# POOL waits for the landing of every third send in a two-layer mixture-of-experts kernel

## What is computed

```python
x = x + 0.5 * _L0_ffn_ref(_layernorm(x), ...)    # pass 0: each token to one of 8 experts
x = x + _L0_attn_ref(_layernorm(x), ...)         # conv, two running means, a gelu layer
x = x + 0.5 * _L0_ffn_ref(_layernorm(x), ...)    # pass 1: the same 8 experts
x = x + 0.5 * _L1_ffn_ref(_layernorm(x), ...)    # 16 experts, 320 places each
x = x + _L1_attn_ref(_layernorm(x), ...)         # a linear scan over the 4096 rows' blocks
x = x + 0.5 * _L1_ffn_ref(_layernorm(x), ...)    # the same 16 experts
```

## Time and profile before

| | us |
|---|---|
| timed runs, median of 3 | 703.73 |
| timed runs, lowest and highest | 702.21, 706.83 |
| profiled execution, first to last instruction | 768.4 |
| PE busy in it | 639.2 |
| POOL busy in it, 377 instructions | 367.9 |

### The profile page before, as it was taken

One profiled execution on the slowest core, in us unless ns is written; L12 is line 12 of the kernel. 1 busy time (PEld: TensorE's weight loads), 2 busy tenths in 40 slices (PEclk: granted clock), 3 DMA queues, 4 the chain that ended last, 5 costly groups with the idle time before them and its releaser, 6 DMA issues.

```text
span 768.4 us, 13116 instructions
## 1 busy us (share of the span) xinstructions
PE 639.2 (83%) x3647; PEld 490.1 (64%) x3647; DVE 449.7 (59%) x1882; ACT 329.6 (43%) x1038; POOL 367.9 (48%) x377
## 2 busy tenths in 40 slices
PE   4451799999989999857997679999997975989996
PEld 4441798986767658756986654576663764466664
DVE  6620456696899987622444330567763875166674
ACT  2220455747866544322553200645531841074551
POOL 0466346345312173554444555366661146445676
PEclk9665899999999999977999769999998997899999
DMA  9661466435103114444767212533397011455330
GB/s 302 234 176 57 124 193 197 114 93 175 61 1 81 43 41 112 140 116 130 189 206 239 69 41 67 177 97 119 110 283 158 13 37 49 116 152 169 99 98 15
DMA packets 85879, 93.95 MB, mean 122 GB/s; under 512 B 12152, under 2 KB 65307, under 8 KB 85552
## 3 DMA queue, kind: packets, MB, share of 16 engines
q1 hardware_dynamic: 73648, 74.23, 33.9%
q0 software_dynamic: 10880, 15.07, 5.9%
q10 hardware_dynamic: 1280, 3.81, 1.5%
HBM read 64.18 MB, written 33.76 MB: 127 GB/s over the span
## 4 chain that ended last, share of the span: by engine, by line
PE 52%; DVE 13%; issue 11%; POOL 7%; another core or an unknown queue 7%; DMA 5%; ACT 3%; SPq 1%; ACTq 0%; DVEq 0%; POOLq 0%
PE ps L901 8%; PE ps L921 8%; PE ps L894 8%; PE ps L821 5%; PE ps L829 5%; POOL y L1610 4%; PE ps L843 3%; PE ps L736 2%; PE ps L876 2%; PE ps L869 2%; POOL xs L1606 2%; PE ps L884 1%; PE ps L778 1%; PE ps L908 1%
## 5 line engine op out<-in xcount | busy, mean ns | idle before, releaser
L1606 POOL DMA_INDIRECT xs<-X,IDX x128 | 125.4, 980 | 143.5 <-issue 70.4
L1499 ACT ACTIVATE ht<-ps,CL 128x128 f32<-128x128 f32 x336 | 93.7, 378 | 136.1 <-PE ps L821 68.1
L1610 POOL DMA_INDIRECT y<-yt,xi x84 | 83.3, 992 | 107.3 <-DVE yt L1242 96.7
L829 PE MATMUL ps<-W,ht 128*128 (+1 forms) x672 | 94.3, 294 | 12.1 <-ACT ht L1499 8.8
L821 PE MATMUL ps<-xt,w1s 128*128 128x128 f32 x672 | 91.8, 291 | 11.4 <-DVE xt L1236 6.2
L829 PEld LDWEIGHTS ps<-W,ht 128*128 128x128 f32 x672 | 86.9, 205 | 18.8 <-issue 17.7
L821 PEld LDWEIGHTS ps<-xt,w1s 128*128 128x128 f32 x672 | 86.4, 205 | 14.0 <-DVE xt L1236 6.5
L921 PE MATMUL ps<-MT,KC 128*128 128x512 f32 x136 | 68.4, 662 | 9.6 <-remote 5.0
L1236 DVE COPY xt<-ps 128x128 f32<-128x128 f32 x84 | 24.1, 287 | 72.9 <-remote 38.4
L921 PEld LDWEIGHTS ps<-MT,KC 128*128 128x128 f32 x136 | 27.9, 212 | 43.9 <-issue 31.5
L811 PE MATMUL ps<-KC,xh 128*128 128x128 f32 x84 | 24.9, 296 | 35.0 <-issue 16.6
(11 more groups left out here) (214 smaller groups left out, 1310.9 us busy)
## 6 DMA issues: line engine op xcount, KB each, us to landing
w1s<-in_w SPq DMA_DIRECT2D x84, 256.0 KB
W<-in_w1x SPq DMA_DIRECT2D x17, 512.0 KB
wx<-in_w1x SPq DMA_DIRECT2D x15, 512.0 KB
X<-y SPq DMA_DIRECT2D x24, 256.0 KB
xs<-ZX SPq DMA_DIRECT2D x32, 185.0 KB
xi<-xs SPq DMA_DIRECT2D x84, 66.0 KB
x<-xs SPq DMA_DIRECT2D x22, 148.0 KB
X<-in_x SPq DMA_DIRECT2D x8, 264.0 KB
```

Source lines behind the costliest of these rows:

```text
L829: r = e.matmul(ps[TILE_BANKS[i % len(TILE_BANKS)]][:, 0:P], HT[i % NHT][:, c, :], W02[:, bass.ds(r0 * F + c * P, P)], start=(c == 0), stop ...
L1499: r = e.activation(HT[i % NHT][:, c, :], ps[TILE_BANKS[i % len(TILE_BANKS)]][:, c * P:(c + 1) * P], ACT.Gelu, bias=CL[:, bass.ds(r0 * 4 + ...
L1606: return e.indirect_dma_start(dst, bass.IndirectOffsetOnAxis(ap=IDX[:, n:n + 1], axis=0), X[:, n, 0:w], None, bounds_check=hi, oob_is_err= ...
L1610: return e.indirect_dma_start(dst, bass.IndirectOffsetOnAxis(ap=ix, axis=0), src, None, bounds_check=hi_home, oob_is_err=False, engine_sem ...
```

## The change

A step called rest is put into POOL's list behind every third send of a row of sends (a row is a stretch of sends and homes without much between them), 40 times in all. A rest makes POOL wait until the send that it issued last has landed. Rests stand behind sends 2 and 5; 8, 11, 14, 17, 20, 23, 26 and 29; 37 and 42; 50; 52, 54, 57, 58, 59 and 61; 64 and 67; 68, 71, 74, 77, 80, 83, 86, 89 and 92; and 98, 101, 104, 107, 110, 113, 116, 119, 122 and 125. Nothing else is added, no instruction is moved on any engine, and the other four lists are the same.

```diff
     "pool": """
-send.0 send.1 send.2 send.3 send.4 send.5 send.6 send.7 send.8 send.9 send.10 send.11 send.12 send.13 send.14 send.15 send.16 send.17 send.18 send.19
+send.0 send.1 send.2 rest.0 send.3 send.4 send.5 rest.1 send.6 send.7 send.8 rest.2 send.9 send.10 send.11 rest.3 send.12 send.13 send.14 rest.4
...
             POOL.wait_ge(sem("pad"), 1)
+            sends, landed = {}, None
             for stage, i in ORDER["pool"]:
-                if stage == "ppow":
+                if stage == "rest":
+                    POOL.wait_ge(sem(landed[0]), landed[1])
+                elif stage == "ppow":
...
-                        send(xs0[p], hi_tile[p], n, ROW).then_inc(sem(f"sent{g - GP.index(p)}"), 16)
+                        name = f"sent{g - GP.index(p)}"
+                        send(xs0[p], hi_tile[p], n, ROW).then_inc(sem(name), 16)
                     else:
...
+                        name = "sentx"
                         send(xs1[p - 2], hi_expert, n, ROWX, sem("issued")).then_inc(sem("sentx"), 16)
+                    sends[name] = sends.get(name, 0) + 16
+                    landed = name, sends[name]
                 elif stage == "home":
...
                     home(y[i >= PASS0[1]], yt[:, :], XI[i % NXI][:, R_ID:ROW].bitcast(U32)).then_inc(sem(f"home{i % NHS}"), 16)
+                    landed = f"home{i % NHS}", turns(i, NHS)
```

More of the change, by code:

```diff
@@ L210 @@
[L210 to L213, removed]
@@ new lines @@
+tturn.73 tup.71 tup.72 tdown.70 tturn.74 tdown.71 tdown.72 tturn.75 tup.73 tturn.76 tup.74 tup.75 tturn.77 tdown.73 tdown.74 tdown.75 pturn.14
+pturn.15 tturn.78 tup.76 pscore.16 tup.77 tdown.76 tturn.79 tup.78 tdown.77 qrank.0 tturn.80 pturn.16 tdown.78 tturn.81 tup.79 tup.80 tturn.82 tup.81
+pscore.17 tdown.79 tturn.83 tdown.80 tdown.81 tup.82 tup.83 tdown.82 qrank.1 tdown.83 pturn.17 pscore.18 pturn.18 pscore.19 qrank.2 warm.0 qrank.3
+pscore.20 warm.1 pturn.19 pturn.20 pturn.21 pscore.21 pscore.22 pscore.23 qrank.4 qrank.5 warm.2 warm.3 qrank.6 warm.4 warm.5 qrank.7 warm.6 warm.7
@@ new lines @@
+warm.8 warm.9 warm.10 warm.11 warm.12 warm.13 warm.14 warm.15 warm.16 warm.17 warm.18 warm.19 warm.20 warm.21 warm.22 warm.23 warm.24 warm.25 warm.26
+warm.27 warm.28 warm.29 warm.30 warm.31 warm.32 warm.33 warm.34 eturn.0 eturn.1 eup.0 eup.1 eup.2 eup.3 eup.4 eup.5 edown.0 eup.6 eup.7 eturn.2
+eback.0 edown.1 eturn.3 eup.8 eup.9 eup.10 eup.11 eup.12 eback.1 eup.13 eup.14 eup.15 eturn.4 edown.2 eup.16 eup.17 eturn.5 eup.18 eback.2 eup.19
+edown.3 eup.20 eturn.6 eback.3 edown.4 eup.21 eup.22 eup.23 eback.4 eup.24 eup.25 eup.26 eup.27 eturn.7 edown.5 eup.28 eup.29 eback.5 edown.6 eturn.8
@@ new lines @@
+rturn.1 rB.0 rB.1 rC1.0 rC2.0 rturn.2 rturn.3 rC1.1 rB.2 rC2.1 pturn.22 pscore.24 rC1.2 rturn.4 rB.3 qrank.8 pturn.23 rC2.2 pscore.25 rC1.3 rB.4
+pturn.24 rturn.5 rC2.3 qrank.9 rC1.4 pscore.26 pturn.25 rturn.6 rB.5 qrank.10 rC2.4 pscore.27 rB.6 pturn.26 rC1.5 rC2.5 rturn.7 pscore.28 qrank.11
+rC1.6 rB.7 rC2.6 qrank.12 pturn.27 pturn.28 pscore.29 rC1.7 pscore.30 rC2.7 qrank.13 qrank.14 pturn.29 pscore.31 qrank.15 warm.50 warm.51 warm.52
+warm.53 warm.54 warm.55 warm.56 warm.57 warm.58 warm.59 warm.60 warm.61 warm.62 warm.63 warm.64 warm.65 warm.66 warm.67 eturn.16 eup.64 eup.65 eup.66
@@ new lines @@
+egexp.31 erela.63""",
+    "pool": """
+send.0 send.1 send.2 rest.0 send.3 send.4 send.5 rest.1 send.6 send.7 send.8 rest.2 send.9 send.10 send.11 rest.3 send.12 send.13 send.14 rest.4
+send.15 send.16 send.17 rest.5 send.18 send.19 send.20 rest.6 send.21 send.22 send.23 rest.7 send.24 send.25 send.26 rest.8 send.27 send.28 send.29
+rest.9 send.30 send.31 home.0 home.1 home.2 home.3 home.4 home.5 home.6 home.7 home.8 home.9 home.10 home.11 home.12 home.13 home.14 home.15 home.16
+home.17 home.18 home.19 apow1.0 home.20 home.21 apow1.1 home.22 home.23 home.24 home.25 home.26 home.27 home.28 apow2.0 apow2.1 home.29 home.30
@@ new lines @@
+home.31 home.32 home.33 home.34 home.35 home.36 apow3.0 home.37 home.38 apow3.1 home.39 home.40 apow1.2 apow1.3 apow1.4 apow1.5 apow2.2 apow1.6
+apow1.7 apow2.3 apow3.2 apow2.4 apow2.5 apow3.3 apow2.6 ppow.0 apow2.7 apow3.4 apow3.5 send.32 send.33 send.34 apow3.6 send.35 send.36 send.37 rest.10
+send.38 send.39 ppow.1 send.40 send.41 send.42 rest.11 send.43 apow3.7 send.44 send.45 send.46 ppow.2 send.47 ppow.3 send.48 send.49 send.50 rest.12
+send.51 home.41 home.42 home.43 home.44 send.52 rest.13 send.53 home.45 home.46 home.47 send.54 rest.14 send.55 send.56 send.57 rest.15 home.48
@@ new lines @@
+home.49 send.58 rest.16 home.50 home.51 send.59 rest.17 send.60 home.52 send.61 rest.18 send.62 send.63 home.53 home.54 home.55 home.56 home.57
+home.58 home.59 home.60 home.61 home.62 home.63 home.64 home.65 home.66 home.67 home.68 home.69 home.70 home.71 home.72 home.73 home.74 home.75
+home.76 home.77 send.64 rest.19 send.65 send.66 send.67 rest.20 home.78 home.79 home.80 home.81 home.82 home.83 send.68 rest.21 send.69 send.70
+send.71 rest.22 send.72 send.73 send.74 rest.23 send.75 send.76 send.77 rest.24 send.78 send.79 send.80 rest.25 send.81 send.82 send.83 rest.26
@@ new lines @@
+send.84 send.85 send.86 rest.27 send.87 send.88 send.89 rest.28 send.90 send.91 send.92 rest.29 send.93 send.94 send.95 epow.0 epow.1 epow.2 epow.3
+epow.4 epow.5 ehome.0 ehome.1 epow.6 ehome.2 epow.7 ehome.3 ehome.4 epow.8 ehome.5 epow.9 ehome.6 epow.10 epow.11 ehome.7 ehome.8 epow.12 epow.13
+ehome.9 epow.14 ehome.10 ehome.11 epow.15 ehome.12 ehome.13 ehome.14 ehome.15 send.96 send.97 send.98 rest.30 send.99 send.100 send.101 rest.31
+send.102 send.103 send.104 rest.32 send.105 send.106 send.107 rest.33 send.108 send.109 send.110 rest.34 send.111 send.112 send.113 rest.35 send.114
@@ L316 @@
+send.115 send.116 rest.36 send.117 send.118 send.119 rest.37 send.120 send.121 send.122 rest.38 send.123 send.124 send.125 rest.39 send.126 send.127
+epow.16 epow.17 epow.18 epow.19 epow.20 epow.21 ehome.16 ehome.17 epow.22 ehome.18 epow.23 ehome.19 ehome.20 epow.24 ehome.21 epow.25 epow.26 ehome.22
+epow.27 ehome.23 epow.28 ehome.24 epow.29 ehome.25 epow.30 ehome.26 epow.31 ehome.27 ehome.28 ehome.29 ehome.30 ehome.31""",
 }
```

141 lines of the change are left out of this document (58 added, 83 removed).

## The result

| us | before | changed |
|---|---|---|
| median of the timed runs | 705.28 | 767.94 |
| lowest, highest | 702.21, 706.90 | 764.90, 772.31 |
| ratio | 1 | 1.09 (1.0861 to 1.094) |
| profiled execution, span | 768.4 | 766.9 |

The change costs 62.7 us; 30 were predicted, and 767.94 lies outside 706 to 751. The profiled execution of the changed kernel took 768.51 us in all, 1.6 us around its span, so its span stands for the timed runs. The trace of before does not, and that became the main question of the study.

The account below looks back on a forecast made before the run. PE was taken as the bound most of the time, POOL's sends in three places. Terms of 13, 2, 8 and 7 us sum to 30, put on the timed median 703.7: 734 us, range 706 to 751.

Parts of the forecast that it names:

- The hold-up belongs to the execution with the profiler on: Late PE results, 54 us of pieces without a releaser, were read as mostly absent from the timed runs.
- A: Pass 0, sends 0 to 31: eight rests in sends 8 to 31 count in full, +13 us.
- B: Pass 1, nine rests: mostly covered by tile work on PE and gaps of POOL, +2 us.
- C: First layer with 16 experts, rests behind sends 64 to 92: partly hidden by a gap, +8 us.
- D: Second layer with 16 experts, sends 96 to 127, ten rests: partly hidden by gaps, +7 us.
- What a rest costs: Inside a row of sends, the next send starts 2.4 us after the last instead of 1.28: 1.1 us per rest.
- A's first rest, +5: Behind send 8 in pass 0: its landing waits for a busy queue, so send 9 starts 5 us later.
- Rests 0 and 1, hidden: Behind sends 2 and 5: hidden because send 8 waits 9.23 us for DVE anyway, so no cost.
- R1: Rival: timed runs have the hold-up too and resting ends it; 699 us (chance 0.13), or 690 with a gain (0.04).
- R2: Rival: waits mostly hidden, 5 us in pass 0 and 5 in the expert layers; 714 us, chance 0.15.
- R3: Rival: pauses also lower PE's clock, costing the expert layers some 8 us each at most; 750 us, chance 0.08.
- What would show it: Signs: sends behind rests 2.4 us later, send 9 near 48, send 31 near 84, profile span about 745.

Follow-up runs that it names:

- e0: The kernel before, unedited, timed and traced once more: 704.74 us beside 704.91, ratio 0.9977.
- e8: The changed kernel with only the rest behind send 8 left, against the kernel before: 711.61 us, ratio 1.008.
- e13: The changed kernel, unchanged, met in the long condition: 783.56 us, ratio 1.0157 against the kernel before at 772.19.
- e1: The changed kernel with only rests 0 to 9 (pass 0) left: 722.71 us against 705.43 for the kernel before, ratio 1.0263.
- e9: The changed kernel with only rests 13 to 18 left: 776.33 us against 774.02 for the kernel before, ratio 1.0001.
- e6: The changed kernel with each of the 40 rests replaced by a small power on POOL that waits for nothing: 732.60 us, ratio 1.0382 against the kernel before.

## Why the prediction was wrong

**The direction** was right, and so was the mechanism where the prediction applied it, in sends 8 to 31: in the timed runs next to nothing hides a row of sends, and what a rest costs POOL goes to the end nearly in full (62.7 of 70.8 us).

**The hold-up belongs to the execution with the profiler on.** Half right. It was not in the timed runs beside it. But it is no effect of the profiler: in the long condition every timed run is as long as that trace, and no trace taken in the short one shows such a piece.

**The step that failed** is that the trace's gaps and slacks were kept after the hold-up had been struck out of it. A was freed of it ("the 13 us count in full"); B kept its cover ("cover: tile work on PE", and POOL's gaps of the earlier trace rows), C and D kept half their gaps ("part of them will be left"), and rests 0 and 1 kept the 9.23 us in front of send 8. Most of this went with the hold-up. In e0 homes follow send 63 every 1.28 us, sends 80, 100, 108 and 116 stand behind 0.30, 1.50, 1.72 and 0.31, and send 8 behind 5.14. The two rests behind sends 64 and 67, put at nothing under C, failed in the same way: they cost POOL 3.6 us, and the gaps that were to cover them, 2.05 and 2.14 us in front of homes 79 and 80 in the trace of before, are 0.30 in e0.

By terms, with what the parts measured alone:

| term | predicted (ends) | measured |
|---|---|---|
| A | 13 (9 to 15) | 17.3 |
| B | 2 (0 to 7) | 18.0, with rests 19 and 20; rests 13 to 18 alone 13.1 |
| C | 8 (5.6 to 10) | 10.5 |
| D | 7 (4.5 to 11) | 10.1 |

A's 17.3 hold rests 0 and 1, which were priced at nothing. B is about half of the miss of 32.7 us. It failed twice: in its cover, and in its price, since six rests cost POOL 13 us there and not 6.6. D stayed below what its rests cost POOL (14.3): the two DVE gaps left in e0, 1.50 and 1.72, are the only cover that the traces show.

**What a rest costs, 1.1 us (1.07 to 1.4).** In an empty stretch it is 1.29: send to send is 2.57 where it was 1.28. SP's 2.35 and 2.43 were too short for POOL; in the changed kernel SP's first load again comes 2.34 behind its send. The 1.29 is within the ends. Beside tile loads it is 2.7 to 3.8 (rests 12 to 15), for which the prediction had no term in B, although it had costed just such a case in A.

**A's first rest, +5.** Measured 4.7: send 9 at 46.01 against 40.02 for send 8. It was right, in a stretch shifted by 2 us, and so was the reason given (q0's case). It is dearer alone: in e8 send 8 starts earlier, at 38.01, and send 9 comes 7.57 us behind it; from 38 to 43 us q0 moved no packet there while q10 moved 1.06 MB. The prediction weighed a rule of the Trainium skill here (DMA: Bandwidth & Descriptors, "Queues, rings and completion order"), under which an engine goes round between its queues packet by packet, and read it as a price of 1.1 us. The runs refute that price. They don't refute the rule: the same sentence of it lets an engine drain a whole packet, of typically 9 to 17 descriptors, before it switches, and no run shows how many the packets of q10 had.

**Rests 0 and 1, hidden.** 2.0 us of 7.2 got through to send 8.

**R1** (the hold-up is in the timed runs too: 699 or 690, that is -5 or -14). In the long condition it could be timed: +11.4. The rests do end the long hold-up in pass 0, as R1 said, and A then costs little (home.40 starts at 181.04 in e13 and 177.99 in the trace of before). Pass 1 costs 9 more by send 63 (365.52 against 353.84), but at send 68 the changed kernel is only 3.6 us behind (437.29 against 433.67). At send 95 it is 9.4 behind (483.98 against 474.59) and at send 127 8.9 (669.98 against 661.11). So what R1 had wrong between these two traces is C, which loses 5.8 us and not the 1.6 that it allowed (10 less 8.45), and A, where it had nothing.

**R2** (714, the waits mostly hidden) is refuted by e1 alone: the rests of pass 0 cost 17.3 us where R2 had 5.

**R3**, the clock: it did fall, and cost nothing that can be seen. The mean granted clock is 0.917 in the changed kernel and 0.955 in e0, lower in the rows of sends, where PE waits anyway. In the four timed runs of the result it lay between 0.911 and 0.935, and their times within 1% of each other. The stretches in which PE sets the pace are as long as before: send 31 to home.40 90.5 us in both (84.25 to 174.76, and 67.46 to 158.03), and ehome.0 to ehome.15 76.3 in both (496.86 to 573.14, and 445.08 to 521.36).

**What would show it.** Sends behind a rest start 2.57 later and not 2.4; send 31 at 84.25 for "near 84"; send 9 at 46.01 for "near 48", since send 8 started 2 us earlier. The span, "about 745", came out at 766.9.

## What to carry to other kernels

Compare a profiled execution's span with the timed median before reading anything else from it. If it is 9% longer, its gaps, slacks and waits belong to another execution than the one to be predicted: either all of them are kept or none, and the thing to do is to ask for the chain as it would be without the odd pieces. A wait for a landing that was three sends old cost nothing measurable here (1.0024); one for the newest costs its whole latency less one issue, and on an engine whose issue sets the pace nearly every such microsecond counts. A ratio holds for the condition that it was taken in: this change is 8 to 9% in the short one (three times) and 1.6% in the long one (once).

## What was not expected of the hardware

- The same kernel takes 705 to 708 us on four chips and 772 to 774 on two others, each met at one time only. In the traces of the latter the waiters of TensorE's results start up to 24.4 us behind the matmul's end (49.75 and 74.19 in e9) while POOL issues indirect transfers every 1.28 us, and less so when POOL pauses every third one (2% of the chain in e13). What does this there, the runs don't show.
- From the start of an indirect send of 128 rows to POOL's next instruction behind its landing are 2.57 us in an empty stretch, up to 5 beside tile loads (342.23 behind 337.18), 6.0 behind send 8, 7.2 behind send 2 and 7.6 in e8.
- A power of 0.89 us put between two sends costs 0.80 us of the row (e6): a little of the 0.30 us of issue hides behind it.
